# Two of ten maxima move from ahead of an attention round into the round itself

## The chip, the cores and the metric

The kernel runs on one core of one Trainium2 chip. The metric is the device time of one execution in microseconds. Before the change the median of three runs is 698.76 us (696.7 to 701.05).

## What is computed

Four layers over `x` of shape (2, 1024, 128): a gated recurrent layer with an MLP, a mixture-of-experts layer with two experts per token, an attention layer, and the mixture of experts again, each added to its input. The change touches the attention layer alone. Cut to what matters, it is this (2 batch rows, 16 heads of 8 columns, 1024 tokens):

```python
attn = softmax(einsum('bhqd,bhkd->bhqk', q, k) * scale, axis=-1)
attn = attn + rel_bias_table[idx].transpose(2, 0, 1)[None]
out  = einsum('bhqk,bhkd->bhqd', attn, v)
out  = layernorm(out) * ln_gamma + ln_beta
```

For the softmax the largest score of each query must be known before the exponentials are taken.

## The kernel before

The eight groups of attention (4 heads of one batch row each) are worked through one after the other. One round of the loop belongs to one group, and two kinds of work run side by side in it.

The first kind is the group's own 16 steps (8 tiles of keys, for each half of the queries). In a step (`step`, line 1505) TensorE makes the four heads' scores (`scores`, line 1476, matmul on line 1487), ScalarE takes the exponentials (line 776), and TensorE weighs the values with the exponentials of the step before (`weigh`, matmul on line 1501). The negated maxima of the queries are carried inside the score matmul, as three extra rows of the operand (59 rows instead of 56). So the first scores of a group wait for `negmax_loaded`.

The second kind is a ring of items that go through two slots of PSUM: TensorE fills a slot (`fill`, line 1452), VectorE empties it (`empty`, line 1103). An item `("max", 1, k)` makes the k-th of 32 score tiles of the *next* group without its maxima (line 1421), and VectorE reduces it to its maxima (line 1079). `("max", 2, k)` does so for the group after the next. Behind the 32nd maximum of the next group VectorE joins its two halves of keys (line 1084); the item `("turn", 1, 0)` transposes the joined maxima on TensorE (line 1428) and splits them into three bf16 parts on VectorE (lines 1090 to 1096); then SP, in `load_negmax`, waits for the last part and issues six small DMAs (line 464) that put them into the next group's operand. `bias`, `bias_turn` and `out` belong to the group itself; the first two occur in the first four rounds alone.

The order of a round's items is the list `RING` (line 198), written out by hand: the maxima of the next group that are left, then the first maximum of the group after, the turn, the other maxima that are taken ahead, and the out item. `EARLY` (line 194) says how many maxima of each group are taken ahead, in the round before. The turn waits on TensorE for the join, and each item for the emptying of its slot; TensorE, VectorE and SP each work in order.

The items are dealt to the 16 steps of a round by position (`beside`, line 1522): step j gets the items from j*n//16 to (j+1)*n//16 of the whole list, where n is 36 in the first four rounds and 34 afterwards. In a step the first of them is filled after the scores of heads 0 and 1, the others after the scores of heads 2 and 3. A round starts with the group's step 2 (`FIRST`) and ends with step 1 of the next group, so the next group's first scores stand at position j = 14 of the 16.

Before the first round `RING_AHEAD` makes all maxima of group 0, its turn and the maxima taken ahead of group 1; the last `BESIDE_FIRST` = `EARLY` - 4 of these run beside steps 0 and 1 of group 0. The round of the last group but one has no group after the next, so its list is shorter (`RING_BEFORE_LAST`), and in it VectorE goes on, after the turn, to the normalization of batch row 0 (`attended_out`, `attended`), which TensorE turns in step 4 of the last group.

Of the kernel before, what the change touches and what calls it, by code (L numbers as in the profile page):

```python
# [190 lines left out]

FIRST = 2

EARLY = 10

NEXT_MAXES = [("max", 1, k) for k in range(EARLY, MAXES)]
AFTER_NEXT = [("max", 2, 0), ("turn", 1, 0)] + [("max", 2, k) for k in range(1, EARLY)]
RING = NEXT_MAXES[:4] + [("bias", 0, 0), NEXT_MAXES[4], ("bias_turn", 0, 0)] + NEXT_MAXES[5:] + AFTER_NEXT + [("out", 0, 0)]

RING_AHEAD = [("max", 1, k) for k in range(MAXES)] + AFTER_NEXT  # L200
BESIDE_FIRST = EARLY - 4

# [1445 lines left out]
```

## Time and profile before

| | |
|---|---|
| median of three runs | 698.76 us |
| profiled execution, own time | 697.31 us |
| its span | 695.5 us |
| mean granted TensorE clock | 0.988 |
| busy TensorE / VectorE / ScalarE / GpSimd | 605.9 / 523.9 / 376.3 / 95.6 us |
| maxima on VectorE (line 1079) | 256 x 1218 ns |
| score matmuls (line 1487) | 512 x 385 ns |
| DMAs of the maxima (line 464) | 48, 4 KB, 1.7 us to landing |

The attention stage runs from about 252 to 620 us of the span. Matmuls are pipelined, so busy TensorE is not TensorE at its peak, and a group of matmuls can end before its last one's modelled end. A wait is put down to what released it last. In the timeline, like instructions of one engine that follow closely are merged into one row with their count; the idle time before a row and its releaser stand in brackets.

### The profile page before, as it was taken

How to read it: one execution, taken by the hardware profiler on the slowest of the kernel's cores; microseconds unless marked ns; L12 is line 12 of the kernel's file. 1: busy time of each engine (PE TensorE's matmuls, PEld its weight loads, DVE VectorE, ACT ScalarE, POOL GpSimd, SP SyncE). 2: the span in 40 equal slices, each digit the busy share in tenths (PEclk: the TensorE clock that was granted, in tenths of full speed). 3: DMA queues.
4: the chain of work that ended last, by engine and by line, in shares of the span. 5: the costliest groups of instructions: out<-in, count | busy, mean ns of one | idle time of the engine just before them, and what ended most of it. 6: DMA issues, size and time to landing. Idle time of an engine off the chain costs nothing.

```text
span 695.5 us, 9222 instructions
## 1 busy us (share of the span) xinstructions
PE 605.9 (87%) x3304; PEld 236.9 (34%) x3304; DVE 523.9 (75%) x958; ACT 376.3 (54%) x692; POOL 95.6 (14%) x96
## 2 busy tenths in 40 slices
PE   7888899899988788888898898888889888887997
PEld 5353545444464542122121121211212112224443
DVE  5657678855769887997978979998998984419734
ACT  3935133333402136776767767787777878762331
POOL 5941120101032802002010000000000011002000
PEclk9999999999999999999999999999999999999999
DMA  8000000000311223003010010010100000000011
GB/s 255 18 1 0 1 0 1 0 1 0 105 60 56 69 66 111 1 22 95 3 36 18 3 52 3 11 46 2 39 16 2 1 2 1 1 1 0 1 30 30
DMA packets 18990, 20.22 MB, mean 29 GB/s; under 512 B 3969, under 2 KB 12673, under 8 KB 18945
## 3 DMA queue, kind: packets, MB, share of 16 engines
q1 hardware_dynamic: 17552, 18.84, 8.7%
q8 instruction: 26, 0.43, 0.3%
q0 software_dynamic: 144, 0.52, 0.2%
q10 hardware_dynamic: 1248, 0.27, 0.2%
q14 instruction: 20, 0.16, 0.1%
HBM read 15.23 MB, written 4.19 MB: 28 GB/s over the span
## 4 chain that ended last, share of the span: by engine, by line
PE 55%; DVE 21%; ACT 11%; SPq 4%; issue 3%; DMA 3%; DVEq 2%; POOL 1%; POOLq 0%; ACTq 0%
PE banks L1501 16%; PE banks L1487 10%; ACT arena L776 8%; DVE negmax L1079 8%; PE banks L1214 6%; PE banks L1292 5%; PE banks L1421 4%; PE banks L1283 3%; SPq L464 3%; PE banks L1335 3%; PE banks L1227 2%; DMA arena<-nm_part 1%; DVE arena L986 1%; PE banks L1436 1%; ACT arena L766 1%
## 5 line engine op out<-in xcount | busy, mean ns | idle before, releaser
L776 ACT ACTIVATE arena<-banks 128x512 f32<-128x512 f32 x512 | 267.7, 604 | 115.9 <-PE banks L1487 115.7
L1079 DVE TENSOR_REDUCE negmax<-banks 128x2 f32<-128x1024 f32 x256 | 299.0, 1218 | 35.3 <-PE banks L1421 33.1
L1487 PE MATMUL banks<-arena 59*128 59x512 bf16 x512 | 139.0, 385 | 31.1 <-ACT arena L776 26.2
L1501 PE MATMUL banks<-arena 128*32 128x512 f32 x1024 | 136.3, 604 | 7.9 <-ACT arena L776 6.6
L1421 PE MATMUL banks<-arena 56*128 56x512 bf16 x512 | 109.7, 383 | 18.9 <-DVE negmax L1079 14.5
L1487 PEld LDWEIGHTS banks<-arena 59*128 59x128 bf16 x512 | 34.3, 93 | 206.9 <-ACT arena L776 183.6
L524 POOL TENSOR_TENSOR rstd<-veps,neghalf 128x4 f32<-128x4 f32 (+1 forms) x24 | 27.1, 1129 | 280.3 <-DVE veps L847 234.9
L1292 PE MATMUL banks<-arena,bT 128*128 128x512 f32 x128 | 60.1, 593 | 1.6 <-ACT arena L619 1.6
L619 ACT ACTIVATE arena<-banks 128x512 f32<-128x512 f32 (+1 forms) x56 | 32.1, 595 | 49.2 <-PE banks L1227 19.2
L933 DVE TENSOR_SCALAR arena<-banks,bi 128x512 f32<-128x512 f32 x32 | 23.9, 745 | 33.1 <-PE banks L1292 33.1
L1421 PEld LDWEIGHTS banks<-arena 56*128 56x128 bf16 x512 | 25.8, 94 | 41.0 <-DVE negmax L1079 34.7
L1501 PEld LDWEIGHTS banks<-arena 128*32 128x32 f32 x1024 | 20.5, 108 | 49.6 <-ACT arena L776 45.7
L1292 PEld LDWEIGHTS banks<-arena,bT 128*128 128x128 f32 x128 | 24.2, 190 | 32.0 <-issue 29.6
L1283 PE MATMUL banks<-hT,wiT 128*128 128x512 f32 x64 | 31.7, 594 | 0.0
L619 ACT ACTIVATE hT<-banks 128x512 f32<-128x512 f32 x12 | 6.7, 598 | 33.5 <-PE banks L1227 33.5
L1543 PE MATMUL banks<-ones,ident 128*128 128x128 f32 x156 | 24.3, 295 | 0.0
L1335 PE MATMUL banks<-arena,woT 128*128 128x512 f32 x48 | 22.1, 597 | 0.3
L1221 PE MATMUL banks<-ones,ident 128*128 128x128 f32 x110 | 16.3, 313 | 6.6 <-POOL ident L515 3.5
L619 ACT ACTIVATE x<-banks,bi 128x512 f32<-128x512 f32 x16 | 11.0, 687 | 20.4 <-PE banks L1292 20.4
L1543 PEld LDWEIGHTS banks<-ones,ident 128*128 128x128 f32 x156 | 19.9, 196 | 5.5 <-issue 5.5
L549 POOL COPY arena<-x 128x256 f32<-128x256 f32 x8 | 3.2, 398 | 131.9 <-PE banks L1421 88.5
L619 ACT ACTIVATE oT<-banks,bo 128x512 f32<-128x512 f32 x8 | 5.5, 687 | 28.5 <-PE banks L1335 28.5
(145 smaller groups left out, 635.6 us busy)
## 6 DMA issues: line engine op xcount, KB each, us to landing
arena<-qk_scratch SPq DMA_DIRECT2D x128, 48.0 KB
arena<-in_tab SPq DMA_DIRECT2D x4, 1024.0 KB, 6.1
qk_scratch<-arena SPq DMA_DIRECT2D x8, 384.0 KB, 2.6
arena<-qk_scratch SPq DMA_DIRECT2D x64, 16.0 KB
out<-x SPq DMA_DIRECT2D x4, 256.0 KB, 2.3
arena<-nm_part SPq DMA_DIRECT2D x48, 4.0 KB, 1.7
x<-in_x POOLq DMA_DIRECT2D x1, 512.0 KB, 7.7
x<-in_x ACTq DMA_DIRECT2D x1, 256.0 KB, 3.8
```

Of the source, the lines that this page charges most:

```text
L524: pool.tensor_tensor(rstd[:, b, h, 0:width], veps[:, b, h, 0:width], neghalf[:, 0:width], ALU.pow).then_inc(rstd_ready, 1)
L619: act.activation(dst, banks[:, BANK[name], :], func, **kw).then_inc(signal or act_emptied, 1)
L776: act.activation(probs[s % 2][:, h, :], score_bank(g, n), ACT.Exp, scale=SCALE).then_inc(exp_done, 1)
L1079: return dve.tensor_reduce(negmax[:, buf, keys, :, at_tile], slot, axis=AXX, op=ALU.max, negate=True)
L1214: last = pe.matmul(banks[:, BANK[name], :], lhsT, rhs, start=i == 0, stop=i == len(terms) - 1)
L1283: pe.matmul(banks[:, BANK[name], :], chunk(wiT, c), half(hT[:, b], h), start=True, stop=False, skip_group_check=True)
L1292: pe.matmul(banks[:, BANK[name], :], chunk(bT, c), half(moe[b][4][:, k, :], h), start=False, stop=k == 1, skip_group_check=True).then_inc( ...
L1335: last = pe.matmul(banks[:, BANK[name], :], woT[:, c, :], moe[b][2][h][:, c, :], start=c == 0, stop=c == FC - 1)
L1421: last = pe.matmul(slot[:, side, :], qs[rows, buf, pair, t * P:(t + 1) * P], ks[rows, buf, pair, keys * HALF:(keys + 1) * HALF], start=Tru ...
L1487: pe.matmul(score_bank(g, n), ks[rows, g % BUFS, pair, t * P:(t + 1) * P], qs[rows, g % BUFS, pair, q * HALF:(q + 1) * HALF], start=True, ...
L1501: last = pe.matmul(pv_bank[32 * h:32 * h + VW, :], vpg[:, g % BUFS, t, h, :], probs[s % 2][:, h, :], start=t == 0, stop=t == NT - 1)
L1543: pe.matmul(pv_bank[:, 0:P], ident[:], ones[:], start=True, stop=True)
```

## The change

One constant goes from 10 to 8. The lists are worked out from it.

```diff
-EARLY = 10
+EARLY = 8

 NEXT_MAXES = [("max", 1, k) for k in range(EARLY, MAXES)]
 AFTER_NEXT = [("max", 2, 0), ("turn", 1, 0)] + [("max", 2, k) for k in range(1, EARLY)]
```

A round begins with the next group's maxima 8 and 9 in front of number 10, and the list no longer has the maxima 8 and 9 of the group after the next in front of the out item. `RING` keeps its 36 items and `RING_PLAIN` its 34; `RING_BEFORE_LAST` goes from 24 to 26; `RING_AHEAD` goes from 43 to 41, and `BESIDE_FIRST` from 6 to 4. In `RING` the bias items keep their positions, the 32nd maximum of the next group goes from position 23 to 25 and the turn from 25 to 27; in `RING_PLAIN` from 21 to 23 and from 23 to 25. The out item stays the last.

## Rows read from the trace of the kernel before

**Rows 1.** Waits of TensorE between 250 and 580 us: waited for, us in total, times, longest

```profile
PE banks L1487 <- ACT arena L776: 21.3, 81, 0.5
...
PE banks L1487 <- DMA arena<-nm_part: 4.2, 6, 1.2
```

**Rows 2.** Chain that ended last, 334 to 352 us: start, us, what

```profile
338.73 1.23 DVE negmax L1079
...
340.05 0.19 DVE joined L1084
...
341.38 0.23 DVE nm_part L1090
...
342.65 0.58 SPq L464
...
346.33 1.73 DMA arena<-nm_part
```

**Rows 3.** Timeline of a 36-item round: start, us, engine, line, idle before

```profile
338.08 0.39 PE L1487 MATMUL banks<-arena 59*128 59x512 bf16 x2
...
340.69 0.39 PE L1487 MATMUL banks<-arena 59*128 59x512 bf16 x2
...
342.65 4.27 SPq L464 DMA_DIRECT2D arena<-nm_part  x6
...
348.12 0.39 PE L1487 MATMUL banks<-arena 59*128 59x512 bf16 x2 [1.24 <-DMA arena<-nm_part]
...
348.65 1.06 PE L1501 MATMUL banks<-arena 128*32 128x512 f32 x8
348.76 1.23 DVE L1079 TENSOR_REDUCE negmax<-banks 128x2 f32<-128x1024 f32 x1 [0.48 <-PE banks L1421]
```

**Rows 4.** Timeline of the first round of 34 items

```profile
481.23 3.73 SPq L464 DMA_DIRECT2D arena<-nm_part  x6
...
486.39 0.38 PE L1487 MATMUL banks<-arena 59*128 59x512 bf16 x1
...
487.55 1.06 PE L1501 MATMUL banks<-arena 128*32 128x512 f32 x8
```

**Rows 5.** Timeline of the round of 24 items

```profile
569.02 4.47 SPq L464 DMA_DIRECT2D arena<-nm_part  x6
...
575.27 1.06 PE L1501 MATMUL banks<-arena 128*32 128x512 f32 x8
...
579.89 2.14 DVE L857 TENSOR_SCALAR nt<-x,mv,rstd 128x128 f32<-128x128 f32 x8 [0.22 <-issue]
...
587.91 1.09 PE L1227 MATMUL banks<-ident,nt 128*128 128x128 f32 x8
```

**Rows 6.** Timeline of the first two steps of the first group

```profile
256.08 1.07 PE L1501 MATMUL banks<-arena 128*32 128x512 f32 x8
...
259.47 1.07 PE L1501 MATMUL banks<-arena 128*32 128x512 f32 x8
```

**Rows 7.** Timeline of TensorE behind idle times elsewhere

```profile
61.55 1.10 PE L1214 MATMUL banks<-hT,mgT 128*128 128x512 f32 x2 [1.99 <-DVE arena L1010]
...
71.83 4.45 PE L1221 MATMUL banks<-ones,ident 128*128 128x128 f32 x25 [3.17 <-DVE arena L1010]
...
196.09 0.39 PE L1421 MATMUL banks<-arena 56*128 56x512 bf16 x2 [2.51 <-DMA arena<-qk_scratch]
```

**Rows 8.** Stretches: us, busy PE, PEld, DVE, ACT, POOL, granted clock, DMA share, GB/s

```profile
62.00:64.00 2.00, 2.00 (x6) 0.95 (x5) 1.89 (x4) 0.63 (x2) 0.00 (x0) 1.00 0.00 0
...
72.00:74.00 2.00, 2.00 (x10) 2.00 (x11) 1.90 (x4) 1.00 (x2) 0.00 (x0) 0.50 0.00 0
...
196.00:198.00 2.00, 1.91 (x12) 1.37 (x13) 1.41 (x2) 0.00 (x0) 0.00 (x0) 0.91 0.23 60
198.00:200.00 2.00, 2.00 (x9) 1.24 (x9) 1.68 (x4) 0.00 (x0) 0.00 (x0) 0.50 0.20 59
200.00:202.00 2.00, 2.00 (x12) 1.48 (x12) 1.76 (x12) 0.00 (x0) 0.00 (x0) 0.73 0.21 68
```

## The prediction

> **What bounds the kernel now.** I read the page first, then the table of what each engine waits for in the attention stage, then the chain of work that ended last through one round, then the timeline of three kinds of round.
>
> The page puts TensorE on more than half of the chain and VectorE on a fifth, so the sum of one engine decides nothing; what counts is which wait ends last in a round. One wait stands out. TensorE's score matmuls (L1487) wait six times for the DMA `arena<-nm_part`, 4.2 us in all, up to 1.2 us; their many waits for ScalarE are a quarter of a microsecond each [rows 1]. This DMA carries the negated maxima of the next group of heads. The chain through it is unbroken [rows 2]: the group's last maximum starts on VectorE at 338.73, the two halves are joined at 340.05, the next ring item, a maximum of the group after, runs, the turned maxima are split from 341.38, SP begins its six issues at 342.65, the last lands 1.73 us after 346.33, and the first scores of the next group start at 348.12; TensorE stood still 1.24 us for them [rows 3]. So in this round whatever makes the last maximum later makes the next group later by as much.
>
> Not every round is like that. Four rounds (the first batch row's groups) have 36 ring items, and there the scores wait. Then follow two rounds of 34 and one of 24. In the first of 34, SP issues at 481.23, and the scores at 486.39 come without a wait [rows 4]. A transfer ends 1.14 us after SP's stretch (346.33 + 1.73 against 342.65 + 4.27) [rows 2, 3], here at 486.10: 0.3 us to spare.
>
> **The change, part by part.** Nothing is computed more or less: 256 maxima before and after, the same six DMAs per group. What moves is order.
>
> *The turn.* Ring items are dealt to the 16 steps of a round by position. With two maxima more in front, the last maximum goes from position 23 to 25 of 36 (21 to 23 of 34), so from step 10 to step 11; the turn from step 11 to step 12; the out item stays last. In the 36-item round the last maximum started 0.65 us after the scores at 338.08; those of the next step come at 340.69, 2.61 us later [rows 2, 3]. VectorE's two extra maxima before it are 2 x 1.2 = 2.4 us of work by the item at 338.73 [rows 2]; that is less than the step, so the step decides: 2.61, lower bound 2.4. From join to SP's issue the same instructions follow, and the six issues and the landing are unchanged, so the scores at 348.12 go to 350.7. TensorE comes there a little later too: the turn, now first in its step, waits for the join and holds up the weighing and the scores queued behind it, and ScalarE's exponentials behind those, by about 0.5 us; that is inside the stall. When the scores resume, VectorE has four maxima and the out item left as before, and it is idle in both cases (it waits 0.48 us now, [rows 3]); nothing is caught up. Four rounds: 4 x 2.61 = **10.4 us**.
>
> *The rounds with slack.* Landing goes from 486.10 to 488.7; scores start 0.05 later, and the weighing 0.53 after them (348.65 - 348.12) [rows 2, 3]: 489.3 instead of 487.55, a loss of 1.7 [rows 4]. The round of 24 items issues at 569.02, for 4.47 instead of 3.73 us: landing at 574.63, later 577.24, weighing at 577.8 instead of 575.27, a loss of 2.5 [rows 5]. The second 34-item round also has such a long stretch of issues; I give it 2.5. Sum **6.7 us**. I don't know why the issues stretch; without it both lose 0.7 less, 5.3 in all.
>
> *The two items that leave the start.* The first two steps of the first group shed a maximum each (three to two). The second step there took 259.47 - 256.08 = 3.39 us against 2.61 of a two-item step [rows 3, 6]: 0.78 each, **-1.6 us**. Bounds: one of them alone, -0.8; both maxima in full, -2.4.
>
> *The two items that come to the end.* The round of 24 becomes 26. VectorE then begins the first batch row's normalization 2.6 later. It ends now at 579.89 + 2.14, and TensorE turns the result at 587.91: 5.9 us of cover, so nothing [rows 5]. Without the cover it would be up to 2.6.
>
> So far 10.4 + 6.7 - 1.6 = **+15.5 us**, between 4 x 2.4 + 5.3 - 2.4 = 12.5 and 10.4 + 6.7 - 0.8 = 16.3.
>
> *The clock.* TensorE's stall per round, now 0.7 us in the mean of six (4.2 / 6) and 1.24 at most, grows by 2.61 less 0.5 in the four rounds, to about 2.8 and 3.4 us; to 2.3 in the first round with slack (488.7 against 486.39), and by the longer issues to about 3 in the other two. The trace has idle times of this size elsewhere. After 1.99 us up to 61.55 the granted clock stayed at 1.00 [rows 7, 8]. After 2.51 us up to 196.09, and after 3.17 us up to 71.83, it fell to 0.50; behind the 2.51 it reads 0.91, 0.50, 0.73 over three stretches of 2 us, which is the 1.2 GHz level for 3.4 us [rows 7, 8]. The missing share is (0.09 + 0.50 + 0.27) x 2 = 1.7 us of full clock; a wait of 0.26 us for ScalarE [rows 1] is absorbed, leaving 1.4, if the low stretch falls on busy steps (lower bound 0, where it falls into the stall itself). By size six of seven stalls lie above 2.51 and one between; one example at 2.51 doesn't make it certain, so I take five: 5 x 1.4 = **+7.0 us**. Bounds: none 0, seven 7 x 1.7 = 11.9.
>
> The Trainium skill, TensorE: Matmul & The Clock Gate, section HAM oscillation, tells of a kernel whose wait for a transfer in every tile drops the clock in every single tile, so that the cost is paid each time anew. By that rule all seven rounds would pay, a rival below; the falls in [rows 7, 8] agree with it, but none of them is in the attention stage.
>
> Sum: 15.5 + 7.0 = +22.5. Against the profiled execution, 697.31 us (span 695.5), that is a span of 718.0 and **719.8 us**; that execution lies 1.45 below the median of the runs shown, from which it would be 721.3. I say 720.
>
> **The rivals.**
> - *The stalls grow and the clock stays* (at most two falls). For it: no fall in the attention stage so far, with stalls of 1.2 us. Against: the fall after 2.51 us. It gives +15.5 to +18, 713 to 715 us; with short issues 711.
> - *The clock falls in every one of the seven rounds* (the rule above). For it: six stalls are longer than one that made it fall. Against: 1.99 us didn't. It gives 15.5 + 7 x 1.4 = +25.3, 722.6 us, up to 726.
> - *Not slower: the later maxima are hidden.* This holds if the landing comes before TensorE is at the scores, from 2.61 us of slack on in a round; the stall then costs nothing and only the start's gain stays: -1.6, 695.7 us. For it: the rounds of 34 items have some slack, 0.3 us before the scores wait. Against: in four rounds TensorE waits for just this transfer already, so there is none.
> - *The turn is late by one item, not by a step*: 1.2 us instead of 2.61, if VectorE had been behind at the last maximum. The landings come 1.4 us earlier than above: 4 x 1.2 + 0.3 + 1.1 + 1.1 - 1.6 = +5.7, 703 us. Against: that maximum started as soon as TensorE had filled it, so the step sets it.
>
> **How the numbers follow.** Falls in three to six rounds: 0.50, the forecast, 718 to 723 us. Clock stays, or falls at most twice: 0.27. All seven: 0.17. One item late: 0.03. Not slower: 0.03. The range reaches from the clock that stays with short issues (711, less 1) to seven falls: 710 to 726. It leaves out the last two cases and little of the others. A change of about 1% (7 us) can be told from none in this kernel: faster 0.01, the same 0.05, slower 0.94.
>
> **What would show it.** In the profile after: the wait of L1487 for `arena<-nm_part` grows from 4.2 us in six waits to about 20 in seven (three of 2.8, one of 3.4, one of 2.3, two of 3); the six issues on SP stay at about 4 us; the chain has this DMA in all seven rounds. The first steps of the first group last 2.6, not 3.4 us. The granted clock reads 0.5 to 0.8 behind some of the stalls, and the mean drops from 0.988 to about 0.975. I am wrong if the scores wait no longer than before, if VectorE turns out to catch up in the last two steps of a round, or if the time grows by 15 us with the clock at 1.00 throughout.

## Result and the profile after

The median after is 725.86 us (722.24 to 729.67, four runs) against 698.96 us (696.7 to 701.05, four runs): a ratio of 1.0386, 95% interval 1.0313 to 1.0459, so 3.9% slower. The profiled execution of the changed kernel took 723.23 us, its span is 721.4 us against 695.5, +25.9; its mean granted clock is 0.958 against 0.988. Of the 22 us of full clock that lie between the two means, 13.7 are missing in the attention stage; 6.9 are missing ahead of it, where the change touches nothing.

The wait foretold is there. This is the table of TensorE's waits of the changed kernel from 250 to 600 us (waited for, us in total, times, longest), the answer to [rows 1]:

```profile
PE banks L1487 <- ACT arena L776: 21.1, 82, 0.5
PE banks L1487 <- DMA arena<-nm_part: 19.2, 7, 3.3
...
PE banks L1428 <- DVE joined L1084: 3.4, 4, 0.8
```

4.2 us in six waits have become 19.2 in seven, and the turn itself (L1428) now waits for the join, 0.84 us in each of the four 36-item rounds. The chain through the second of these rounds, the one of [rows 2]:

```profile
346.06 1.23 DVE negmax L1079
...
347.38 0.19 DVE joined L1084
347.57 1.14 DVE negmax L1079
...
353.07 1.73 DMA arena<-nm_part
```

Its parts are those of before. From the last maximum to SP's first issue at 349.93 pass 3.87 us (before: 342.65 - 338.73 = 3.92), and from there to the scores at 354.85 pass 4.92 (before 5.47, with one long issue among the six). What changed is where the last maximum stands against TensorE's steps. The timeline of the same round, the answer to [rows 3]:

```profile
345.41 0.39 PE L1487 MATMUL banks<-arena 59*128 59x512 bf16 x2
...
347.72 0.27 PE L1428 MATMUL banks<-ident,joined 128*32 128x128 f32 x1 [0.84 <-DVE joined L1084]
...
349.93 3.73 SPq L464 DMA_DIRECT2D arena<-nm_part  x6
...
354.85 0.39 PE L1487 MATMUL banks<-arena 59*128 59x512 bf16 x2 [2.72 <-DMA arena<-nm_part]
...
355.39 1.06 PE L1501 MATMUL banks<-arena 128*32 128x512 f32 x8
355.50 1.23 DVE L1079 TENSOR_REDUCE negmax<-banks 128x2 f32<-128x1024 f32 x1 [2.10 <-PE banks L1421]
```

The last maximum starts 0.65 us after the scores of step 11 (345.41); before, it was 0.65 behind those of step 10. TensorE stands 2.72 us for the transfer, and VectorE, out of items, 2.10 us with it. Nothing is caught up.

The rounds with slack follow. First the timeline of the first round of 34 items, the answer to [rows 4], and then that of the round of 26 (24 before), the answer to [rows 5]:

```profile
500.28 1.07 PE L1501 MATMUL banks<-arena 128*32 128x512 f32 x8
...
505.24 0.39 PE L1487 MATMUL banks<-arena 59*128 59x512 bf16 x2 [3.35 <-DMA arena<-nm_part]
...
505.77 1.07 PE L1501 MATMUL banks<-arena 128*32 128x512 f32 x8
...
594.60 1.06 PE L1501 MATMUL banks<-arena 128*32 128x512 f32 x8
...
598.33 0.39 PE L1487 MATMUL banks<-arena 59*128 59x512 bf16 x2 [2.34 <-DMA arena<-nm_part]
...
598.64 1.48 PE L1501 MATMUL banks<-arena 128*32 128x512 f32 x8
...
604.35 2.14 DVE L857 TENSOR_SCALAR nt<-x,mv,rstd 128x128 f32<-128x128 f32 x8 [0.22 <-issue]
...
613.81 0.44 PE L1227 MATMUL banks<-ident,nt 128*128 128x128 f32 x2
```

Weighing to weighing this step takes 5.49 us in the first (before 2.61, the length of an unhindered step) and 4.04 in the second (before 2.56). The two items that came to the end cost nothing: the normalization ends at 606.5 and TensorE turns it at 613.8.

Then the clock. These are 2 us stretches of the changed kernel behind the seven waits (columns as in [rows 8]):

```profile
302.00:304.00 2.00, 1.26 (x8) 0.33 (x12) 0.18 (x1) 0.56 (x2) 0.00 (x0) 0.55 0.01 2
304.00:306.00 2.00, 2.00 (x12) 0.16 (x5) 1.04 (x1) 0.53 (x2) 0.00 (x0) 0.50 0.00 0
306.00:308.00 2.00, 2.00 (x12) 0.41 (x12) 1.29 (x2) 1.79 (x4) 0.00 (x0) 0.50 0.00 0
308.00:310.00 2.00, 2.00 (x13) 0.22 (x10) 1.16 (x1) 0.95 (x3) 0.00 (x0) 0.74 0.03 8
...
356.00:358.00 2.00, 1.75 (x16) 0.32 (x8) 1.69 (x2) 1.61 (x4) 0.00 (x0) 1.00 0.00 0
...
404.00:406.00 2.00, 1.11 (x8) 0.29 (x12) 0.04 (x1) 0.41 (x1) 0.00 (x0) 0.65 0.01 2
406.00:408.00 2.00, 2.00 (x10) 0.18 (x8) 1.19 (x1) 0.67 (x2) 0.00 (x0) 0.50 0.00 0
...
457.00:459.00 2.00, 2.00 (x10) 0.20 (x8) 1.23 (x1) 1.08 (x2) 0.00 (x0) 0.50 0.00 0
...
506.00:508.00 2.00, 1.75 (x15) 0.32 (x8) 1.69 (x2) 1.61 (x4) 0.00 (x0) 1.00 0.01 4
...
553.00:555.00 2.00, 2.00 (x13) 0.28 (x5) 0.58 (x1) 0.31 (x2) 0.00 (x0) 0.55 0.00 0
...
601.00:603.00 2.00, 1.74 (x7) 1.20 (x7) 1.78 (x13) 2.00 (x5) 0.27 (x1) 0.50 0.00 0
```

It fell to the 1.2 GHz level behind five of the seven waits. Behind the first the missing share is (0.45 + 0.50 + 0.50 + 0.26) x 2 = 3.4 us of full clock, twice what [rows 8] showed; behind the wait at 404.89, (0.35 + 0.50) x 2 = 1.7. Behind the longest wait of all (3.35 us, up to 505.24) it stayed at 1.00.

The score waits end at 302.74, 354.85, 404.89 and 456.35 in the first four rounds (before: 300.09, 348.12, 395.60, 443.08). The timeline of the changed kernel at two of them, and then that of the kernel before at the third:

```profile
302.74 0.61 PE L1487 MATMUL banks<-arena 59*128 59x512 bf16 x2 [2.72 <-DMA arena<-nm_part]
...
404.89 0.60 PE L1487 MATMUL banks<-arena 59*128 59x512 bf16 x2 [2.72 <-DMA arena<-nm_part]
```

```profile
395.60 0.39 PE L1487 MATMUL banks<-arena 59*128 59x512 bf16 x2 [0.70 <-DMA arena<-nm_part]
```

This prices the two parts apart. From 354.85 to 404.89 the clock stayed up: 50.04 us against 47.48, +2.56 for the later landing alone. From 404.89 to 456.35, with one single fall, 51.46: 1.4 more. From 302.74 to 354.85, with a double one, 52.11 against 48.03, which held a long issue of 0.54: 4.62, so 2.1 for the clock.

### The profile page after: what moved, and what is told of

Its sections match the earlier page's. It is cut to its first block, busy times and chain, and to the rows that moved or that the text cites. A ratio compares the mean times of both kernels' runs of the same rounds, so it can differ in the third digit from the quotient of the medians.

```text
span 721.4 us, 9222 instructions
## 1 busy us (share of the span) xinstructions
PE 621.8 (86%) x3304; PEld 239.8 (33%) x3304; DVE 525.8 (73%) x958; ACT 376.1 (52%) x692; POOL 96.3 (13%) x96
## 4 chain that ended last, share of the span: by engine, by line
PE 56%; DVE 19%; ACT 11%; SPq 4%; DMA 4%; issue 3%; DVEq 2%; ACTq 0%; POOLq 0%; POOL 0%
PE banks L1501 16%; PE banks L1487 10%; ACT arena L776 8%; DVE negmax L1079 7%; PE banks L1214 6%; PE banks L1292 5%; PE banks L1421 5%; SPq L464 3%; PE banks L1283 3%; PE banks L1335 3%; DMA arena<-nm_part 2%; PE banks L1227 2%; PE banks L1543 1%; DVE arena L986 1%; PE banks L1436 1%
## 5 line engine op out<-in xcount | busy, mean ns | idle before, releaser
L1487 PE MATMUL banks<-arena 59*128 59x512 bf16 x512 | 143.4, 395 | 46.3 <-ACT arena L776 26.2
L1501 PE MATMUL banks<-arena 128*32 128x512 f32 x1024 | 142.1, 628 | 6.9 <-ACT arena L776 5.8
L1421 PE MATMUL banks<-arena 56*128 56x512 bf16 x512 | 114.2, 397 | 13.6 <-DVE negmax L1079 10.5
L1543 PE MATMUL banks<-ones,ident 128*128 128x128 f32 x156 | 26.0, 309 | 0.0
L1543 PEld LDWEIGHTS banks<-ones,ident 128*128 128x128 f32 x156 | 21.5, 209 | 6.1 <-issue 6.1
L532 POOL TENSOR_SCALAR z<-x,mv,rstd 128x128 f32<-128x128 f32 x16 | 21.1, 1331 | 0.0
L828 DVE BATCH_NORM_STATS2 stats<-x 128x6 f32<-128x128 f32 x80 | 17.4, 280 | 4.2 <-DMA x<-in_x 3.3
```

What stands on the lines that cost most here:

```text
L1421: last = pe.matmul(slot[:, side, :], qs[rows, buf, pair, t * P:(t + 1) * P], ks[rows, buf, pair, keys * HALF:(keys + 1) * HALF], start=Tru ...
L1487: pe.matmul(score_bank(g, n), ks[rows, g % BUFS, pair, t * P:(t + 1) * P], qs[rows, g % BUFS, pair, q * HALF:(q + 1) * HALF], start=True, ...
L1501: last = pe.matmul(pv_bank[32 * h:32 * h + VW, :], vpg[:, g % BUFS, t, h, :], probs[s % 2][:, h, :], start=t == 0, stop=t == NT - 1)
L1543: pe.matmul(pv_bank[:, 0:P], ident[:], ones[:], start=True, stop=True)
```

## Experiments

The theory: a later turn makes the transfer of the maxima land behind TensorE's arrival at the scores, one step later per two positions, and the stalls then drop TensorE's clock. Its main rivals: the two maxima cost by their new place; the stall alone costs and the lower clock nothing.

**The turn late, the maxima where they were** (`e1_turn_late`). Only the turn moves in the ring.

```diff
-AFTER_NEXT = [("max", 2, 0), ("turn", 1, 0)] + [("max", 2, k) for k in range(1, EARLY)]
+AHEAD_NEXT = [("max", 2, 0), ("turn", 1, 0)] + [("max", 2, k) for k in range(1, EARLY)]
+AFTER_NEXT = [("max", 2, k) for k in range(3)] + [("turn", 1, 0)] + [("max", 2, k) for k in range(3, EARLY)]
...
-RING_AHEAD = [("max", 1, k) for k in range(MAXES)] + AFTER_NEXT
+RING_AHEAD = [("max", 1, k) for k in range(MAXES)] + AHEAD_NEXT
```

> Ten maxima are taken ahead as in the kernel before, and the two stay where they were; only the turn stands two items later in the rounds (behind three maxima of the group after the next instead of one), so at the same positions as in the changed kernel. Theory (the turn's lateness is the cost): the splits come 2.4 to 2.6 us later in each round, the scores wait about 19 us in seven waits instead of 4.2 in six, the clock falls behind several of them; without the gain of 1.6 us at the start the time is 725 to 729 us. Rival (the two maxima cost by their new place at the head of the round, as work of VectorE and TensorE): they have not moved, so 699 us with 4 us of waits.

Measured: 724.57 us, ratio 1.0337 (1.028 to 1.0394). The waits for the transfer, in the table of TensorE's waits of this kernel (its lines are one further down):

```profile
PE banks L1488 <- DMA arena<-nm_part: 18.9, 7, 2.8
```

This is the changed kernel's loss, as far as the two intervals can tell, with EARLY still at 10 and without moving a single maximum across a round; the median lies just under the 725 to 729 us expected. The turn's later place is enough for the loss. It waits here for VectorE to empty its slot (0.47 us a round), and in the changed kernel for the join (0.84); both times two maxima more stand ahead of it. The clock fell behind six of these seven waits.

**The stall filled** (`e2_fill`, `e7_fill8`). TensorE computes something nobody reads while it would wait; 16 or 8 matmuls.

```diff
+                if n == 0 and G > 0:
+                    pe.wait_ge(exp_done, at(G, exp_done, -2))
+                    for _ in range(16):
+                        pe.matmul(score_bank(g, 0)[:, 0:P], ident[:], ones[:], start=True, stop=True)
                 if n == 0:
                     pe.wait_ge(negmax_loaded, at(G, negmax_loaded, 16 * NPART * SIDES))
```

> The changed kernel, and in each group after the first TensorE makes 16 matmuls of 128 columns that nobody reads (1.9 us at full clock) into the score bank before it waits for the maxima. Theory (the waiting costs 16.5 us and the lower clock behind it 9 us more): the waits that are left are 0.3 to 1.5 us, the granted clock of the attention stage is 1.00, its mean 0.985 to 0.99, and the time is 699 + 17 = 716 us. Rival (the lower clock costs nothing, since a round is held by the transfer anyway): the clock is as high, but the time stays at 726 us. Second rival (the fillers themselves delay the scores): above 726.

Measured: 721.32 us, ratio 1.031 (1.0285 to 1.0334). No theory had this number; the second rival was right in its mechanism, since the fillers ran longer than the stall, and wrong in its time. In the timeline of this kernel (a filler shows as two matmuls):

```profile
299.79 3.84 PE L1482 MATMUL banks<-ones,ident 128*128 128x128 f32 x32
303.56 0.39 PE L1491 MATMUL banks<-arena 59*128 59x512 bf16 x2
```

I had taken 1.9 us for 16 of them; they took 3.84, and TensorE no longer waited but came late by itself (303.56 against 302.74 in the changed kernel). Even so the median is 4.5 us under the changed kernel's, with a granted clock of 1.00 in the whole attention stage; the two intervals just overlap. The price of the clock was still open, and the half number was run.

> As the kernel with 16 fillers, with 8: those took 3.84 us of each stall and so were longer than the stall of 2.72; eight take about 1.9 us. Theory (the lower clock is about a third of the loss): waits of 0.8 us are left, the granted clock of the attention stage is 1.00 or nearly, and the time is 714 to 717 us. Rival (the lower clock costs nothing): 721 us or more, as with 16 fillers, since the transfer sets the round.

Measured: 713.58 us, ratio 1.0211 (1.0178 to 1.0244). The timeline of one round of this kernel:

```profile
348.56 2.05 PE L1482 MATMUL banks<-ones,ident 128*128 128x128 f32 x16
351.36 0.39 PE L1491 MATMUL banks<-arena 59*128 59x512 bf16 x2 [0.75 <-DMA arena<-nm_part]
```

Its table of TensorE's waits, where the fillers have taken the place of most of the 19.2 us:

```profile
PE banks L1491 <- DMA arena<-nm_part: 4.9, 7, 1.5
```

And its engines over a stretch of 50 us (columns as in [rows 8]):

```profile
300.00:350.00 50.00, 43.86 (x319) 12.12 (x318) 40.95 (x44) 34.24 (x66) 4.44 (x4) 1.00 0.14 41
```

The clock reads 1.00 in every such stretch up to 600 us. The scores still wait for the transfer: the first four waits end at 301.32, 351.36, 401.40 and 451.44, 50.04 us apart, just as long as the changed kernel's one round without a fall, so the fillers cost nothing there. The median is 12.3 us lower (725.86 - 713.58). So of the change's 27 us some 15 are the later landing, less the gain at the start (713.58 against 698.91), and some 12 the lower clock behind it; the intervals of the two ratios leave 7 to 18 us for the clock.

**The chain cut** (`e3_parts`). VectorE signals each part, and SP doesn't wait for the third before it issues the first.

```diff
-                dve.tensor_copy(nm_part[:, 0, :], rows)
+                dve.tensor_copy(nm_part[:, 0, :], rows).then_inc(negmax_split, 1)
...
-                sp.wait_ge(negmax_split, at(G, negmax_split, 1))
                 for i in range(NPART):
+                    sp.wait_ge(negmax_split, at(G, negmax_split, i + 1))
```

> The changed kernel, but VectorE signals each of the three parts of the split maxima, and SP issues the two DMAs of a part as soon as that part is there, so that the issues begin about 1.0 us earlier (341.65 instead of 342.65 in the round shown of before). Theory (the scores wait for this chain alone): each of the seven waits is 1.0 us shorter, 12 us in all instead of 19; with fewer falls of the clock the time is 708 to 717 us. Rival (TensorE and VectorE are late by themselves, and the transfer only lands last): the waits shrink and the time stays within 2 us of 726.

Measured: 711.53 us, ratio 1.0187 (1.0147 to 1.0228). The timeline of the second round of this kernel, SP's issues and TensorE's scores:

```profile
346.90 3.74 SPq L464 DMA_DIRECT2D arena<-nm_part  x6
...
351.82 0.39 PE L1487 MATMUL banks<-arena 59*128 59x512 bf16 x2 [1.71 <-DMA arena<-nm_part]
```

And its table of TensorE's waits:

```profile
PE banks L1487 <- DMA arena<-nm_part: 13.8, 7, 2.9
```

SP begins 0.30 us behind the start of the first cast (346.60) instead of 1.31 behind it, and this round's wait is 1.01 us shorter than the changed kernel's (1.71 against 2.72). The sum falls by 5.4, not 7: most of the rest is missing in the last three rounds, where one transfer landed late (the wait of 2.9) and two stretches of issues took 4.36 and 4.34 us, against 4.13 and 3.66 in the changed kernel. The median falls by 14.3 us, more than the waits: the clock fell behind three of the seven waits in the profile (0.50 from 304 and from 404 us, 0.54 from 498), not five.

**Two positions further** (`e6_early6`). The rest of the ring follows from this number.

```diff
-EARLY = 8
+EARLY = 6
```

> Six instead of eight maxima are taken ahead: the turn another two positions later, in step 13. Theory (one step per two positions): each of the seven waits is 2.6 us longer again, about 37 us in all, the clock falls behind every one; the start gains nothing more, since a step with one item is as long as one with two. 726 + 18 + 2 to 5 = 746 to 749 us. Rival (the loss comes from one boundary that the turn passed, and is paid once per round): 726 to 730 us.

Measured: 744.93 us, ratio 1.0655 (1.0619 to 1.069). The timeline of this kernel at the scores of the second round:

```profile
358.50 0.61 PE L1487 MATMUL banks<-arena 59*128 59x512 bf16 x2 [5.25 <-DMA arena<-nm_part]
```

And its table of TensorE's waits:

```profile
PE banks L1487 <- DMA arena<-nm_part: 36.5, 7, 5.8
```

2.5 us more in this round (5.25 against 2.72), 17.3 in all, and the clock fell behind all seven. The time is 1 us under the range expected and far from the rival's: the loss goes on with the next two positions, it is no single boundary.

**Two positions beyond the kernel before** (`e8_early12`).

```diff
-EARLY = 8
+EARLY = 12
```

> Twelve instead of ten maxima are taken ahead: the turn two positions earlier, in step 10, so that the transfer lands 2.6 us earlier than in the kernel before. Theory (the loss begins where the landing comes behind TensorE's arrival): no wait for the transfer is left, which gives back at most 0.25 us a round and 0.8 in one, 1.5 in all; the first two steps of the first group have a maximum more each and lose 1.6 to 2.4 us. 698 to 702 us, the same as before. Rival (each maximum taken ahead is worth something, 13 us apiece as between ten and eight): 675 to 690 us.

Measured: 704.62 us, ratio 1.0076 (1.0049 to 1.0103), 0.8% slower than before the change, and above what was expected. No wait for the transfer is left in the table of its waits, so the theory of the landing holds, but the start was dearer. The timeline of its first steps, and a weighing of the last group:

```profile
254.07 0.39 PE L1487 MATMUL banks<-arena 59*128 59x512 bf16 x2
...
268.45 1.06 PE L1501 MATMUL banks<-arena 128*32 128x512 f32 x8
...
610.06 1.93 PE L1501 MATMUL banks<-arena 128*32 128x512 f32 x8
```

And that of the kernel before, the same first scores and third weighing:

```profile
252.69 0.39 PE L1487 MATMUL banks<-arena 59*128 59x512 bf16 x2
...
262.08 1.07 PE L1501 MATMUL banks<-arena 128*32 128x512 f32 x8
```

A stretch among the first steps, with the granted clock third from the end (columns as in [rows 8]):

```profile
258.00:260.00 2.00, 1.74 (x10) 0.31 (x10) 2.00 (x3) 0.86 (x2) 0.00 (x0) 0.50 0.00 0
```

From the first scores to the third weighing 14.4 us pass, against 9.4 before (252.69 to 262.08): TensorE waits for slots of the ring, with four maxima in a step instead of three, and in this execution it did so at the lower clock. How much of the 5 us is the fourth maximum and how much the clock, this run doesn't tell. The clock fell a second time, from about 609 to 616 us (the weighing at 610.06 takes 1.93 us instead of 1.06), and behind the first steps the execution lost 1.9 us more. TensorE had waited for no transfer before either fall: in the 8 us before them its longest waits were 0.74 us, for a slot, and 0.59 us, for ScalarE.

**The chain cut in the kernel before, and cut twice** (`e9_parts10`, `e10_parts_pool8`, `e11_parts_pool9`). The first is `e3_parts` with ten maxima ahead; the others, with eight and nine, also give three of the six DMAs to GpSimd's queue.

```diff
+            def load_side_1(G, buf):
+                for i in range(NPART):
+                    pool.wait_ge(negmax_split, at(G, negmax_split, i + 1))
+                    row = SIDE + STACK + i
+                    pool.dma_start(qs[row:row + 1, buf, :, :].rearrange("o h (t q) -> o (h t) q", q=P),
+                                   nm_part[PAIRS * NT:2 * PAIRS * NT, i, :]).then_inc(side_1_loaded, 16)
```

> The kernel before (ten maxima ahead) with the six issues begun as soon as the first part is split, 1.0 us earlier. Theory: the waits of 0.7 us in four rounds go, which costs 0.25 us a round now, 1.0 to 2 us in all: 697 to 699 us, not to be told from the kernel before. Rival (the chain of the maxima holds every round): 4 x 1.0 us and more, below 696 us.

Measured: 697.54 us, ratio 0.9976 (0.9956 to 0.9996). One wait of 0.2 us is left:

```profile
PE banks L1487 <- DMA arena<-nm_part: 0.2, 1, 0.2
```

> The changed kernel with the chain cut further: the issues begin as soon as a part is split, SP issues the three DMAs of one side and GpSimd's queue, idle then, the three of the other. If GpSimd issues as fast as SP (0.6 us each), the last landing comes 2.9 us earlier than in the changed kernel. Theory (slack decides, not the number of maxima ahead): the waits of 2.7 us shrink to 0 to 0.3 us (one or two longer ones where an issue stretches), the clock stays up, the start keeps its gain of 1.6 us, and the turn's own wait for the join stays (0.84 us in four rounds): 697 to 702 us, as before the change. Rival (GpSimd's issues or landings are slower than SP's): each wait is longer by that, up to the 726 us of the changed kernel.

Measured: 698.49 us, ratio 1.0000 (0.9978 to 1.0021). The timeline of one round of this kernel, SP's issues and GpSimd's:

```profile
344.83 1.85 SPq L464 DMA_DIRECT2D arena<-nm_part  x3
...
345.11 0.51 POOL L586 DMA_DIRECT2D arena<-nm_part  x1 [25.58 <-DVE nm_part L1100]
345.79 0.98 POOL L586 DMA_DIRECT2D arena<-nm_part  x2 [0.17 <-issue]
```

And its table of TensorE's waits:

```profile
PE banks L1498 <- DMA arena<-nm_part: 1.6, 3, 0.7
```

Eight maxima ahead, with the turn as late as in the changed kernel, and the loss is gone to within the interval (0.2%, 1.5 us), since the transfer starts earlier and is issued in half the time. GpSimd issues about as fast as SP here. The Trainium skill, Trainium Kernel Development and Optimization, section Key Constraints, says that issuing from several engines only saves the sequencers' issue time; the trace agrees (a stretch of 1.85 instead of 3.73 us), and in this kernel just that time stood on the path.

> Nine maxima ahead, with the split chain on two queues (SP and GpSimd). The turn stands one position later than with ten, which costs at most one step, 2.6 us; the chain is 2.9 us shorter, so no wait should be left, and the start has one maximum less beside it: 0.8 us of gain. Theory (slack decides): 1 to 2.5 us faster than the kernel before, 696.5 to 698 us, about as the kernel with ten ahead and the issues begun early (697.5). Rival (fewer maxima ahead cost something besides the wait for the transfer): 700 us and more.

Measured: 698.65 us, ratio 0.9994 (0.9980 to 1.0008), with no wait for the transfer: the same as before, and the foretold gain of 1 to 2.5 us (696.5 to 698) isn't there. Where waits are gone, one maximum more or less ahead can't be told apart. `e9_parts10` is the best of all, by 0.2%, at the edge of what its runs can tell.

## Why the prediction was right, and where it was short

The median, 725.86 us, lies 5.9 us above the 720 forecast and outside the 718 to 723 of the main case. It is inside the range by 0.14 us, and two of the four runs (728.49 and 729.67) are above its end. The path and the sum of the waits were right; that the range held was luck, since the clock's term was too small.

- *The path.* Right: the transfer of the maxima, which already held the scores in four rounds, holds them in all seven, 19.2 us in seven waits where about 20 were foretold. `e1_turn_late` shows that the later turn is enough, and `e10_parts_pool8` that nothing is left of the loss, as far as its runs can tell, once the transfer lands in time.
- *The turn in four rounds, +10.4.* The rows give 2.56 a round. One long issue of 0.54 us that stood in the round of [rows 3] didn't recur, so 4 x 2.56 - 0.54 = 9.7.
- *The rounds with slack, +6.7.* 5.49 - 2.61 = 2.9 in the first (I said 1.7; the landing came 2.3 us behind SP's stretch, not 1.14), 4.04 - 2.56 = 1.5 in the last (2.5; its issues took 3.66, not 4.47). The middle one, by the same weighings, 2.5. In all 6.9: the parts were off, and the sum was right by luck.
- *The start, -1.6.* Right. The weighings of the first group's first steps in the changed kernel, the answer to [rows 6]:

```profile
256.97 1.06 PE L1501 MATMUL banks<-arena 128*32 128x512 f32 x8
...
259.58 1.06 PE L1501 MATMUL banks<-arena 128*32 128x512 f32 x8
```

2.61 us apart instead of 3.39, and the first 2.58 us behind the first scores (254.39) instead of 3.39 (252.69).
- *The clock, +7.0.* This is the term that was too small. Five falls were taken and five came in the profiled execution, but they cost 1.8 us each in the mean, not 1.4: the low stretch was twice as long behind three of them. The rounds with falls lose 2.1, 1.4, 2.1, 1.1 and 2.5 us, 9.2 in all (the last is what is left to the end of the span); by the medians of the kernel with eight fillers it is 12. The slower two of the four runs have a lower mean granted clock (0.948 and 0.951 against 0.956 and 0.958), so they may hold more or longer falls than the profiled one; there is no trace of those runs. The way to the number was weak too. I sorted the stalls by size, and size doesn't decide: 3.35 us didn't lower the clock; in `e3_parts` it fell behind a wait of 1.72 and stayed up behind waits of 1.71 and 2.00; in `e8_early12` it fell with none above 0.74 shortly before.
- *The rest.* TensorE's first scores came 1.7 us later in this execution (254.39 against 252.69), before anything that the change touches; in the traces on record they come between 252.60 and 254.67, whatever the kernel, and low-clock stretches ahead of the attention stage differ between the executions. 9.7 + 6.9 - 1.6 + 9.2 + 1.7 = 25.9, the difference of the spans.
- *The rivals.* "The clock stays" gave 713 to 715 us; with eight fillers, which make just that case, it is 713.6. "The clock falls in all seven", 722.6 up to 726, is nearest to the median, though the profile shows five falls rather than seven, three of them longer. The rule behind it (the Trainium skill, TensorE: Matmul & The Clock Gate, section HAM oscillation: the cost is paid in every tile anew) agrees with `e6_early6`, where all seven waits of about 5 us made it fall; of the changed kernel's waits, 2.3 to 3.4 us, two of seven didn't. "Not slower" and "one item late" found nothing for them.

## What to carry to other kernels

In a loop whose engines wait for each other through a short chain (here maxima, join, turn, split, six issues, landing), the position of the chain's first link in a hand-written order was worth a whole step of the loop here, so look for the slack at its end before work is pushed in front of it (2.6 us per round for each step of lateness). Count a stall on TensorE twice: once for its length and once for the clock behind it, which was nearly as much here (some 12 against some 15 us), and try fillers a little shorter than the stall to tell them apart (2.05 us of them in a stall of 2.72 cost nothing, 3.84 us did). Shortening the chain, by signalling each part as it is ready and issuing from two queues, gave back all that the later turn cost, as far as the runs can tell.

## What the hardware showed that was not expected

- The low clock behind a stall lasted 3.4 us in one place and twice that in another, and in `e1_turn_late` it stayed from 302 to about 312 us; it followed no length of a stall that I could see. Waits of 2.72 us lowered the clock in three rounds and left it up in a fourth, and in `e8_early12` it fell twice with no wait above 0.74 us shortly before. What decides it stays open.
- At the lower clock a weighing's eight matmuls took 1.93 us instead of 1.06, but a round lost only 1.1 to 2.5 us, where 1.7 or 3.4 us of full clock were missing. In the low stretches TensorE reads busy for 2.00 of 2 us (304 to 308 us), at full clock for 1.75 (356 to 358), so part of the missing clock goes into waits that it has anyway, among them those for ScalarE's exponentials.
- SP's six issues of 4 KB took 3.66 to 4.47 us as they stood, 0.6 us each as a rule, and from one issue to the landing 1.7 us passed as a rule, up to 2.9 in the kernels before and after and up to 3.5 in `e3_parts`. The end of this chain has that much jitter.
